# Four engines' instruction streams as hardware loops instead of written out, in a macaron transformer kernel on one core

## The chip, the core and the metric

The kernel runs on one core of a Trainium2 chip. A core has five engines with a program each: TensorE (PE, whose weight loads are listed as PEld), VectorE (DVE), ScalarE (ACT), GpSimd (POOL) and SyncE (SP), which here issues DMAs. They meet only through semaphores: an instruction adds to one when it is done, another waits until it has reached a value. The metric is the device time of one execution in microseconds (us), lower is better. The kernel before took 3411.37 us (median of 3 runs, 3408.09 to 3413.0).

## What is computed

The input `x` is 2 x 1024 tokens of 128 numbers in float32. The reference, cut to what matters:

```python
x = x + 0.5 * ffn_ref(layernorm(x))      # 6 layers, below
x = x + attn_ref(layernorm(x))           # h = x @ w_in.T + b_in; y[t] = sigmoid(a) * y[t-1] + b * h[t]; y @ w_out.T + b_out
x = x + 0.5 * ffn_ref(layernorm(x))      # the same 6 layers again

def ffn_ref(x):
    for i in range(6):
        x = attn_layer(shift_tokens(x), Wqkv[i], q_scale[i], k_scale[i], Wo[i]) + x
        x = ffn_layer(shift_tokens(x), ln_g[i], ln_b[i], W1[i], b1[i], W2[i], b2[i]) + x
```

`shift_tokens` takes the second half of the features from the token before. `attn_layer` projects to q, k and v (16 heads of 64), scales q and k to length 1 by head, multiplies by learned scales, rotates them with a scaled rotary table, and lets each block of 32 tokens attend to itself and the block before it, with a mask and a softmax; the result goes through `Wo`. `ffn_layer` is a layer norm, `W1` to a value and a gate of 341 each, value times gelu(gate), and `W2`.

## The kernel before

The 2048 tokens are 16 tiles of 128, and the 12 layers make 192 tiles of work (`T`; `N` = 96 for each six layers). All layers run through one software pipeline. Its step `s` works on tile `s - lag` in each stage; the lags are `L_X` 0 (the shifted input, transposed), `L_QKV` 1 (projection of q and k, sums of squares, rotation), `L_S` 2 (transposes of q and k, values, scores), `L_SM` 3 (softmax), `L_AV` and `L_WO` 4 (attention times values, output projection), `L_F` 5 and `L_F2` 6 (the feed-forward half). Tile `u` of the next layer enters 16 steps after tile `u` of this one. Around step 96 the recurrence between the two halves is worked in (`middle`, lags 7 to 12).

Each engine has its own function `step(k)`, which emits this engine's instructions for one step in a fixed order; the order and the waits are written by hand. A `Step` object `k` stands for one step. In a step that is written out `k.reg` is None: tile numbers, addresses and the values that waits compare with are constants. In a step of a hardware loop `k.reg` is the loop's register; `k.val` and `k.off` then compute each count and address with register instructions at the place where it is first needed in the loop's body, and keep it for later uses in the same body (`memo`). A few waits are emitted only in written-out steps.

The part of a step that the prediction follows:

- TensorE: `project(k, 1)` and `project(k, 0)` (L503) fill both halves of the PSUM tensor `proj`. Behind the transposes of q and the attention come `project(k, 2)` and `project(k, 3)`. Further on come the output projection (L606), the transposes of the probabilities (L614), `values(k, 1)` and `values(k, 0)` (L509), again into `proj`, the transpose of the next input (L652), `hidden` (L522), the mask (L532) and the scores (L540). `values(k, 0)` waits for `v_ab[2]`, VectorE's last rotation, which reads the same half of `proj`.
- ScalarE: `square` (L705) of projections 1 and 0 into `sq`, Exp of the scores (L718), copies of q and of the attention's result, squares 3 and 2, further copies out of PSUM, and Gelu of the gate (L769). The compiler puts an ACT_TABLE_LOAD ahead of a function where the table at hand doesn't hold it.
- VectorE: from `a_sq[0]` on, `rotate(k, c, ...)` multiplies a projection by `tab` twice, into `swp` (L895) and `rot` (L901). Between these stand the row sum of the softmax (L986), its reciprocal (L995) and the sums of squares (L1000, L1003). The inverse root of these is a chain of small operations that ends in `rn` (L882). Then come hT, value times gate (L1037), the row maximum (L1044), its subtraction (L1047) and the statistics of the layer norm (L1052).
- GpSimd: the power for the layer norm (L1114), the softmax's scaling (L1118), `swp` + `rot` (L1124) and its scaling by `rn` (L1133).
- SyncE: four DMAs each for the shifted `xs` and `xs2`, two for `vb`, and in even steps a chunk of the next layer's `wq` and `wo`.

TensorE runs through `pipeline_by_layer`: a prologue, loops of two steps by layer, and a middle that is written out. The other four run through `pipeline`, which in this kernel writes out every step.

Of the kernel before, what the change touches and what calls it, by code (L numbers as in the profile page):

```python
# [47 lines left out]
FRONT = 6  # L48
UNROLL = 2
MID, MID_END = N - TILES + M_X - 1, N + M_Z  # L50
# [6 lines left out]
def macaron(nc, x_in, w_in, b_in, a_in, b_gain, w_out, b_out, w_qkv, q_scale, k_scale, w_o,  # L57
            ln_g, ln_b, w_1, b_1, w_2, b_2, c_rope, c_mask, c_ident, out):
    with ExitStack() as ctx:
# [221 lines left out]
        def unrolled(eng, step, first, end, between=None):  # L281

            for s in range(first, end):
                step(Step(eng, None, s, {}))
                if between is not None:
                    between(s)

        def looped(eng, step, first, end, layer=None):

            odd = first % 2  # L290
            assert (end - first) % UNROLL == 0
            with eng.Fori(first - odd, end - odd, UNROLL) as i:
                memo = {}
                for j in range(UNROLL):
                    step(Step(eng, i, odd + j, memo, layer))

        def pipeline(eng, step, between=None, mid_end=MID_END, end=T, last=T + L_F2):

            unrolled(eng, step, 0, FRONT, between)
            unrolled(eng, step, FRONT, last)  # L300


        def pipeline_by_layer(eng, step, between=None):
# [59 lines left out]
        def _(sp):  # L363
# [114 lines left out]

            sp.wait_ge(c_zero2, 1)
            pipeline(sp, step, between, mid_end=N + TILES, end=OUT - 1, last=OUT + TILES)  # L480
            sp.wait_ge(d_out, 16 * TILES)
            sp.wait_ge(d_wq, 16 * (CHUNKS * LAYERS + FIRST_Q - W_Q // 2))
# [217 lines left out]
        def _(act):  # L700
# [110 lines left out]
            act.wait_ge(c_zero, 1)  # L811
            act.wait_ge(c_zero2, 1)
            pipeline(act, step, between)


        @block.vector
        def _(dve):
# [269 lines left out]

            dve.wait_ge(c_zero, 1)
            pipeline(dve, step, between, end=OUT - 1)


# [141 lines left out]
```

## Time and profile before

| | |
|---|---|
| median of 3 runs | 3411.37 us |
| the profiled execution | 3411.37 us, of which the span from first to last instruction is 3409.5 |
| TensorE busy | 3280.2 us (96%) |
| VectorE busy | 2808.3 us (82%) |
| ScalarE busy | 2425.1 us (71%) |
| GpSimd busy | 2202.4 us (65%) |
| mean granted TensorE clock | 0.993 of full speed |

Busy time is that of the operations on data. Instructions that only compute registers, branch, wait for a semaphore or issue a DMA are not counted; the view of one source line lists them, with the engine's name and a q (PEldq, DVEq). Where a view names a releaser behind an idle time, it is the instruction whose semaphore ended it; "issue" stands where it shows none.

### The profile page before, as it was taken

The page shows a single profiled execution, that of the slowest core. Times are in us where ns is not written, and L with a number is a line of the kernel's source. Part 1 is how long each engine was busy: PE and PEld are TensorE (multiplying, and loading weights), DVE is VectorE, ACT ScalarE, POOL GpSimd, SP SyncE. Part 2 cuts the span into 40 slices and gives each one's busy share as a digit, 9 for nine tenths or more (in the row PEclk, how much of TensorE's full clock was granted, in tenths as well). Part 3 has the DMA queues.
Part 4 walks back from the last instruction along what each step waited for, and adds up shares of the span by engine and source line. Part 5 has one row for each costly group of instructions (what it writes and reads, how often), then busy time and mean ns, then how long its engine had stood idle before and what let it go on. Part 6 is the DMA issues. An engine that isn't in the chain of part 4 may idle for free. (4 is left out here: it accounts for less than half of the span.)

```text
span 3409.5 us, 154564 instructions
## 1 busy us (share of the span) xinstructions
PE 3280.2 (96%) x63324; PEld 2477.0 (73%) x63515; DVE 2808.3 (82%) x6984; ACT 2425.1 (71%) x3769; POOL 2202.4 (65%) x1422
## 2 busy tenths in 40 slices
PE   6999999999999999999999999999999999999998
PEld 4677777777777777777666777777777777777776
DVE  5788888888888888889999887888888888888885
ACT  2777777777777777777666777777777777777775
POOL 4666666666666666667666666666666666666664
PEclk7999999999999999999999999999999999999999
DMA  3111111111111111111111111111111111111111
GB/s 114 50 45 48 46 48 45 46 48 45 48 46 48 45 49 45 45 48 47 46 41 42 48 45 49 45 48 46 48 45 46 47 45 48 45 48 45 51 49 43
DMA packets 198817, 164.11 MB, mean 48 GB/s; under 512 B 139610, under 2 KB 172525, under 8 KB 198509
## 3 DMA queue, kind: packets, MB, share of 16 engines
q1 hardware_dynamic: 193901, 157.05, 16.8%
q10 hardware_dynamic: 4608, 3.34, 0.3%
q8 instruction: 146, 2.39, 0.3%
q14 instruction: 162, 1.33, 0.1%
HBM read 33.38 MB, written 1.05 MB: 10 GB/s over the span
## 5 line engine op out<-in xcount | busy, mean ns | idle before, releaser
L1124 POOL TENSOR_TENSOR rot<-rot,swp 128x1024 f32<-128x1024 f32 x384 | 907.6, 2364 | 140.3 <-DVE rot L901 140.3
L503 PE MATMUL proj<-wq,xsT 128*128 (+1 forms) x1536 | 778.9, 627 | 76.3 <-DMA wq<-in_L_ffn_Wqkv 37.7
L705 ACT ACTIVATE sq<-proj 128x512 f32<-128x512 f32 x768 | 437.7, 596 | 575.6 <-PE proj L503 565.1
L1133 POOL TENSOR_TENSOR rot<-rot,rn 128x1024 f32<-128x1024 f32 x384 | 724.4, 1908 | 0.0
L1114 POOL TENSOR_TENSOR rt<-rt,half 128x1 f32<-128x1 f32 x192 | 105.3, 548 | 855.6 <-DVE rt L983 855.6
L895 DVE TENSOR_TENSOR swp<-proj,tab 128x512 f32<-128x512 f32 x768 | 524.2, 683 | 53.5 <-issue 34.4
L901 DVE TENSOR_TENSOR rot<-proj,tab 128x512 f32<-128x512 f32 x768 | 519.2, 676 | 2.2 <-PE tps L514 2.2
L514 PEld LDWEIGHTS tps<-idf,rot 128*128 128x128 f32 x3072 | 362.6, 142 | 208.8 <-issue 204.7
L1037 DVE SCALAR_TENSOR_TENSOR hT<-proj,b1c,fg 114x128 f32<-114x128 f32 (+1 forms) x576 | 166.7, 345 | 418.2 <-ACT fg L769 412.2
L1118 POOL TENSOR_TENSOR prob<-prob,rr 128x1024 f32<-128x1024 f32 x192 | 365.4, 1903 | 187.2 <-DVE rr L995 187.2
L503 PEld LDWEIGHTS proj<-wq,xsT 128*128 128x128 f32 x1536 | 260.0, 191 | 311.5 <-issue 242.2
L540 PEld LDWEIGHTS sps<-kT,qT 64*32 64x32 f32 x24576 | 357.4, 106 | 88.7 <-issue 88.5
L514 PE MATMUL tps<-idf,rot 128*128 128x128 f32 x3072 | 401.9, 274 | 4.0 <-POOL rot L1133 2.3
L540 PE MATMUL sps<-kT,qT 64*32 64x64 f32 x24576 | 389.8, 217 | 6.0 <-issue 6.0
L509 PE MATMUL proj<-wq,xsT 128*128 (+1 forms) x768 | 391.2, 604 | 2.5 <-DVE rot L901 2.2
L555 PE MATMUL ops<-pT,vb 64*64 64x32 f32 x12288 | 376.4, 221 | 1.7 <-issue 1.5
L606 PE MATMUL ops<-wo,oT 128*128 (+1 forms) x3072 | 374.6, 276 | 2.4 <-ACT oT L727 2.4
L555 PE MATMUL ops<-pT,va 64*64 64x32 f32 x12288 | 372.1, 219 | 1.2 <-issue 1.1
L606 PEld LDWEIGHTS ops<-wo,oT 128*128 128x128 f32 x3072 | 358.2, 192 | 2.6 <-issue 2.6
L555 PEld LDWEIGHTS ops<-pT,vb 64*64 64x64 f32 x12288 | 327.2, 135 | 34.6 <-issue 34.2
L555 PEld LDWEIGHTS ops<-pT,va 64*64 64x64 f32 x12288 | 328.0, 135 | 1.7 <-issue 1.6
L522 PEld LDWEIGHTS proj<-xnT,w 128*114 128x114 f32 (+1 forms) x2304 | 267.9, 178 | 82.8 <-issue 77.5
(113 smaller groups left out, 5683.5 us busy)
## 6 DMA issues: line engine op xcount, KB each, us to landing
vb<-va SPq DMA_DIRECT2D x192, 384.0 KB, 3.5
vb<-va SPq DMA_DIRECT2D x192, 128.0 KB, 3.4
wq<-in_L_ffn_Wqkv SPq DMA_DIRECT2D x95, 192.0 KB
xs<-Z SPq DMA_DIRECT2D x384, 32.0 KB
xs<-Z SPq DMA_DIRECT2D x384, 28.0 KB
xs<-Z SPq DMA_DIRECT2D x384, 3.8 KB
xs<-Z SPq DMA_DIRECT2D x384, 0.2 KB
wo<-in_L_ffn_Wo SPq DMA_DIRECT2D x94, 64.0 KB
```

The lines of the kernel that those rows point to most:

```text
L503: mm(proj[:, c % 2, :], xsT[:, k.parity(L_QKV), :], wq2[:, bass.ds(w + c * 512, 512)], start=True, stop=True).then_inc(p_qkv[c], 1)
L509: mm(proj[:, c, :], xsT[:, k.parity(L_S), :], wq2[:, bass.ds(w + (4 + c) * 512, 512)], start=True, stop=True).then_inc(p_v[c], 1)
L514: last = tr(tps[:, p, :], rot[:, g * INNER + p * P:g * INNER + (p + 1) * P], idf[:, :])
L540: last = mm(sps[to:to + WIN, ty, p * 64:p * 64 + 64], qT[rows, p, w * WIN:(w + 1) * WIN], kT[rows, p, at:at + 2 * WIN], start=False, stop= ...
L555: last = mm(o4[hp * DH:(hp + 1) * DH, g, :], v, pT[rows, p, to:to + WIN], start=True, stop=True, skip_group_check=True)
L606: last = mm(ops[:, 0, 0:P], oT[:, p, :], wo[:, bass.ds(w + p * P, P)], start=(p == 0), stop=(p == PAIRS - 1))
L705: fn(sq[:, c * 512:(c + 1) * 512], proj[:, c % 2, :], ACT.Square).then_inc(a_sq[c], 1)
L895: v.tensor_tensor(halves(swp[:, c * 512:(c + 1) * 512]), swapped, tab[:, bass.ds(po + (2 * g + 1) * POS * DH, DH)] .rearrange("p (a d) -> ...
L901: v.tensor_tensor(heads(rot[:, c * 512:(c + 1) * 512]), heads(src), tab[:, bass.ds(po + 2 * g * POS * DH, DH)].unsqueeze(1) .to_broadcast( ...
L1118: g_.tensor_tensor(pr, pr, rr[:, :].unsqueeze(2).to_broadcast([P, HEADS, 2 * WIN]), ALU.mult).then_inc(g_nrm, 1)
L1124: g_.tensor_tensor(r, r, swp[:, g * INNER:(g + 1) * INNER], ALU.add).then_inc(g_add[g], 1)
L1133: g_.tensor_tensor(r, r, rn[:, g * HEADS:(g + 1) * HEADS].unsqueeze(2) .to_broadcast([P, HEADS, DH]), ALU.mult).then_inc(g_nm[g], 1)
```

## The change

`pipeline` puts two stretches of steps into hardware loops, with two steps in a loop's body (`UNROLL` = 2). `FRONT` is 6, `MID` 86, `MID_END` 108 and `T` 192. `pipeline_by_layer`, and so TensorE's program, isn't touched. Line numbers behind it grow by 3.

```diff
         def pipeline(eng, step, between=None, mid_end=MID_END, end=T, last=T + L_F2):
 
             unrolled(eng, step, 0, FRONT, between)
-            unrolled(eng, step, FRONT, last)
+            looped(eng, step, FRONT, MID)
+            unrolled(eng, step, MID, mid_end)
+            looped(eng, step, mid_end, end)
+            unrolled(eng, step, end, last)
```

ScalarE and GpSimd loop over steps 6 to 85 and 108 to 191, VectorE over 6 to 85 and 108 to 181 (`end` is `OUT - 1`), SyncE over 6 to 85 and 112 to 181. `looped` was there before, for TensorE:

```python
with eng.Fori(first - odd, end - odd, UNROLL) as i:
    memo = {}
    for j in range(UNROLL):
        step(Step(eng, i, odd + j, memo, layer))
```

With it the instructions on the four engines change. ScalarE at the start of a step, written out (`sq` is the square, `prob` the Exp, `qT` the copy of q):

```order
L705 ACTIVATE sq<-proj 128x512 [waits p_qkv1,v_red0]
L705 ACTIVATE sq<-proj 128x512 [waits p_qkv0]
L718 ACT_TABLE_LOAD
L718 ACTIVATE prob<-prob 128x1024 [waits v_sub]
L723 COPY qT<-tps 128x1024 [waits p_S,p_qT]
```

The same place in the first step of a loop's body, an even step:

```order
L292 ISA
L708 ACT_TABLE_LOAD [waits p_qkv1]
L708 ACTIVATE sq<-proj 128x512 [waits v_red0]
L708 ACTIVATE sq<-proj 128x512 [waits p_qkv0]
L224 REGISTER_ALU
L721 ACTIVATE prob<-prob 128x1024 [waits v_sub]
L726 COPY qT<-tps 128x1024 [waits p_S,p_qT]
```

The table load stands ahead of the first square now, behind the wait for `p_qkv1`, and there is none at the Exp. In the body's second step it stands at the Exp, as before. ISA and REGISTER_ALU are register instructions; an ISA row is a fused one that does several.

ScalarE at the Gelu, written out:

```order
L709 COPY va<-proj 128x512 [waits p_v0]
L769 ACT_TABLE_LOAD [waits v_h]
L769 ACTIVATE fg<-proj,b1c 114x128 [waits p_f1]
L769 ACTIVATE fg<-proj,b1c 114x128
L769 ACTIVATE fg<-proj,b1c 113x128
```

And in the loop:

```order
L712 COPY va<-proj 128x512 [waits p_v0]
L772 ISA [waits v_h,p_f1]
L772 ACT_TABLE_LOAD
L772 ACTIVATE fg<-proj,b1c 114x128
L772 ISA
L772 ACTIVATE fg<-proj,b1c 114x128
```

The wait for `p_f1`, the gate's half of `hidden`, stood behind the table load and stands ahead of it now.

VectorE at the start of a step, from the statistics of the layer norm on, written out:

```order
L1052 BN_STATS st<-xs 128x6 [waits d_xs2]
L895 TENSOR_TENSOR swp<-proj,tab 128x512 [waits g_add0,a_sq0,g_tab]
L901 TENSOR_TENSOR rot<-proj,tab 128x512 [waits p_qT,a_sq0]
L895 TENSOR_TENSOR swp<-proj,tab 128x512 [waits g_add0,a_sq1,v_bn]
L978 BN_AGGR mv<-st 128x2
```

And in the loop, at the body's second step:

```order
L1055 BN_STATS st<-xs 128x6 [waits d_xs2]
L224 REGISTER_ALU [waits g_tab]
L898 ISA [waits g_add0,a_sq0]
L898 ISA
L898 TENSOR_TENSOR swp<-proj,tab 128x512
L904 ISA [waits p_qT,a_sq0]
L904 TENSOR_TENSOR rot<-proj,tab 128x512
L898 TENSOR_TENSOR swp<-proj,tab 128x512 [waits g_add0,a_sq1,v_bn]
```

Between the arrival of `a_sq0` and the first product stand two fused register instructions, which work out the place in `tab`.

## Rows read from the trace of the kernel before

**Rows 1.** The page: busy us by engine, share of the span, instructions.

```profile
PE 3280.2 (96%) x63324; PEld 2477.0 (73%) x63515; DVE 2808.3 (82%) x6984; ACT 2425.1 (71%) x3769; POOL 2202.4 (65%) x1422
```

**Rows 2.** Waits: engine, line, releaser, us in total, times, longest.

```profile
ACT sq L705 <- PE proj L503: 565.1, 413, 6.4
...
DVE swp L895 <- issue: 34.4, 78, 1.1
...
PEld proj L509 <- DVE rot L901: 8.6, 23, 1.1
```

**Rows 3.** TensorE's weight loads in time: start, busy us, idle before; three step starts.

```profile
2004.45 0.30 PEld L503 LDWEIGHTS proj<-wq,xsT 128*128 128x128 f32 x2 [0.27 <-issue]
...
2016.24 0.30 PEld L509 LDWEIGHTS proj<-wq,xsT 128*128 128x128 f32 x2
...
2017.41 1.37 PEld L522 LDWEIGHTS proj<-xnT,w 128*114 128x114 f32 x12 [0.49 <-issue]
2018.78 0.14 PEld L532 LDWEIGHTS sps<-mask,idb 128*128 128x128 bf16 x2
...
2021.84 0.30 PEld L503 LDWEIGHTS proj<-wq,xsT 128*128 128x128 f32 x2 [0.65 <-issue]
...
2038.80 0.30 PEld L503 LDWEIGHTS proj<-wq,xsT 128*128 128x128 f32 x2 [0.27 <-issue]
```

**Rows 4.** ScalarE in time, in the same even step.

```profile
2005.67 0.60 ACT L705 ACTIVATE sq<-proj 128x512 f32<-128x512 f32 x1 [2.32 <-PE proj L503]
2006.47 0.60 ACT L705 ACTIVATE sq<-proj 128x512 f32<-128x512 f32 x1 [0.20 <-PE proj L503]
2007.09 1.28 ACT L718 ACT_TABLE_LOAD   x1
...
2011.32 1.08 ACT L705 ACTIVATE sq<-proj 128x512 f32<-128x512 f32 x2
...
2018.01 1.28 ACT L769 ACT_TABLE_LOAD   x1
```

**Rows 5.** VectorE in time, in that step and at the start of the next.

```profile
2007.16 0.69 DVE L895 TENSOR_TENSOR swp<-proj,tab 128x512 f32<-128x512 f32 x1
...
2010.93 0.25 DVE L995 RECIPROCAL rr<-rs 128x16 f32<-128x16 f32 x1
2011.10 1.17 DVE L1000 TENSOR_REDUCE sps<-sq 128x16 f32<-128x1024 f32 x1
...
2015.38 0.68 DVE L901 TENSOR_TENSOR rot<-proj,tab 128x512 f32<-128x512 f32 x1
...
2017.67 0.19 DVE L882 SCALAR_TENSOR_TENSOR rn<-rt,sps 128x32 f32<-128x32 f32 x1
2020.29 0.87 DVE L1037 SCALAR_TENSOR_TENSOR hT<-proj,b1c,fg 114x128 f32<-114x128 f32 x3 [2.43 <-ACT fg L769]
2021.43 1.23 DVE L1044 TENSOR_REDUCE mx<-sps 128x16 f32<-128x1024 f32 x1 [0.28 <-PE sps L540]
...
2024.55 0.69 DVE L895 TENSOR_TENSOR swp<-proj,tab 128x512 f32<-128x512 f32 x1 [0.43 <-issue]
```

**Rows 6.** ScalarE's table loads at the Exp: count, us busy, mean ns.

```profile
L718 ACT ACT_TABLE_LOAD x189 | 242.5, 1283 | 3.3
```

**Rows 7.** Control instructions of TensorE's queue by source line: count, ns min/median/max.

```profile
L224 PEldq ALU_OP  x640: 32/32/42, 131.6 to 3311.7; - x160
...
L292 PEldq COMPARE_BRANCH  x80: 81/216/262, 166.5 to 3328.3; - x80
...
L532 PEldq FUSED_REGOPS  x160: 107/110/120, 145.9 to 3325.9; - x160
```

**Rows 8.** The page's DMA queues for instructions: packets, MB.

```profile
q8 instruction: 146, 2.39, 0.3%
q14 instruction: 162, 1.33, 0.1%
```

**Rows 9.** A small transfer: KB, us from issue to landing.

```profile
out<-xb SPq DMA_DIRECT2D x16, 64.0 KB, 1.8
```

## The prediction

> **What bounds the kernel now.** I read the views in this order: the page's busy shares, the waits, the order of time of one step on TensorE, the same step on ScalarE and VectorE, and last the rows of the control instructions that the busy shares leave out.
>
> The shares name TensorE: 3280.2 us, 96% of the span [rows 1]. The waits show the others idle, ScalarE for 565.1 us before its squares [rows 2], and VectorE stands 2.43 us before hT in a step [rows 5]. Read so, ScalarE and VectorE have 2 to 3 us to spare in each step and more instructions on them would cost nothing. The step itself says otherwise. TensorE's loads for `project` start at 2004.45, 2021.84 and 2038.80 [rows 3]: 17.39 us for the even step, 16.96 for the odd one, 34.35 a pair. Inside the even step:
> - `project` starts at 2004.45; ScalarE squares its two halves at 2005.67 and 2006.47, each 0.60 long [rows 3, 4]. The second ends at 2007.07.
> - VectorE takes it up at 2007.16, 0.09 later, and 17 more operations run behind it without idle time until the last rotation ends, 2015.38 + 0.68 = 2016.06 [rows 5].
> - TensorE's load for `values(k, 0)`, which must wait for that rotation (its PSUM bank is the one that the rotation reads), starts at 2016.24 [rows 3], 0.18 after it. After it come the transpose, `hidden`, the mask, the scores and the next `project` in a row [rows 3].
>
> So 2.62 + 0.09 + 8.90 + 0.18 = 11.8 us of the 17.4 are a chain over ScalarE and VectorE, and the rest is TensorE's own. The chain closes on itself in every step. TensorE looks busy only because its own work over those 11.8 us (projections, transposes, attention, output projection) happens to be as long as the chain; it has hardly any wait there to give (8.6 us in 23 waits of L509 for the rotation) [rows 2]. A microsecond added between a `project` and the last rotation is a microsecond on the period. ScalarE's and VectorE's idle times lie elsewhere: 2.32 us before the first square, in which ScalarE can do nothing for this tile, and the 2.43 us before hT.
>
> The Trainium skill ("Perfetto Trace Analysis", "Identifying the Most-Contended Engine") says to take the engine of highest occupancy as the one that binds, and, for TensorE, to distrust the matmul share. By its first half a change that leaves TensorE's program alone leaves 3411 us; this trace disagrees, by the 0.18 us between the rotation and the load.
>
> **The change part by part.** TensorE's program stays the same. Steps 6 to 85 (40 turns of two steps) and from 108 on become loops: 42 turns on ScalarE and GpSimd, 37 on VectorE, 35 on SyncE, whose second loop starts at 112. The prologue, the middle (22 steps around the recurrence, 26 on SyncE) and the last steps stay written out.
>
> 1. *The table load changes place.* Written out, ScalarE loads a table before each Exp (189 loads of 1283 ns) and one before each Gelu [rows 4, 6]; Square follows Gelu without one. At 2007.09 to 2008.37 the Exp's load lies behind both squares, and the row sum that waits for Exp comes late enough not to see it. In the loop the first instruction with a function is the Square of the even step; the program order puts a load there, behind the wait for `p_qkv1`, and none before the Exp of that step. In the odd step the load stays at Exp. So in 42 + 40 = 82 even steps the first square starts 1.28 us later. The second used to wait for its half until 2006.47, 0.80 after the first; back to back it follows by about 0.49 (two squares take 1.08 us) [rows 4]. Its end moves by 1.28 + 0.02 + 0.49 - 0.80 = 1.0 us. This lies on the chain: 1.0 x 82 = 82 us.
>
> 2. *Control instructions in front of VectorE's first product.* In the loop the `tab` offset is worked out behind the wait for `a_sq0`: two fused register instructions, then `swp`. Nothing covers them, since all else waits for the same square. No row of VectorE has such an instruction. Nearest are TensorE's: ALU_OP 32 ns, the fused one for the mask 110 ns, a compare-and-branch 216 [rows 7]. The two here compute several values each, as the 110 ns one does. With a little for the passage from one to the next I take 0.15 each, 0.3 us a step, in even and odd steps.
>
> 3. *Control instructions behind the row sum.* In the even step the count for `g_nrm` is computed behind the wait for `v_sum`, and a fused instruction stands between the reciprocal and the first reduction (2010.93 and 2011.10) [rows 5]. The reciprocal lasts 0.25, so it hides about one of the three. I take 0.28. In the odd step the counts are known: 0.
>
> 4. *Those that are covered.* The address and count instructions before the other products and reductions lie under operations of 0.68 to 1.22 us; the loop's back edge (the branch is 0.22 on TensorE, the whole turn 0.65 - 0.27 = 0.38 before its loads) [rows 3, 7] on VectorE lies under L1047's operation, which is as long as L1044's 1.23 us [rows 5], and on ScalarE in its 2.32 us of idleness [rows 4]. In the rsqrt chain an operation of 0.19 us waits for the one before; one register instruction fits beside each, and the three around the Z update add some 0.4 us to rn (2017.67 + 0.19 = 2017.86) [rows 5]. The mask's load is at 2018.78 [rows 3], 0.9 later, so 0.4 is covered; if each cost 0.22 it would be 0.9 and just show.
>    ScalarE's Gelu load now stands behind the wait for `p_f1` and not before it: it ran at 2018.01, while `hidden` ran from 2017.41 [rows 3, 4]. It moves by about 0.4, hT by 0.6 with its own fused instructions. hT ended at 2020.29 + 0.87 = 2021.16, its follower began at 2021.43, so 0.3 comes through to L1047 and BN_STATS. In the even step the later square covers that; in the odd one VectorE was idle 0.43 us before `swp` [rows 5]. Cost 0, with 0.1 us to spare.
>    GpSimd is busy for 65% of the span and late nowhere on the chain, and SyncE's ten DMA issues of a step have whole steps until they are read, so their address instructions cost nothing; without that cover theirs would be about 0.1 us each on xs2.
>
> Sum: even 1.0 + 0.3 + 0.28 = 1.58, odd 0.3, a pair 1.88, with 0.9 of it from VectorE. 82 x 1.0 + 77 x 0.9 = 82 + 69 = 151 us. The profiled execution took 3411.37 us, 1.9 more than its span, and is itself the median of the runs. 3411 + 151 = **3562 us**, 4.4% slower.
>
> Bounds: seven control instructions of a pair are exposed (two, two, and three). At 0.032 us (an ALU_OP) they are 0.2 a pair, at 0.216 (the branch) 1.5: 82 + 15 = 97 to 82 + 116 = 198 us, 3508 to 3609. I lie between, near the fused rows, since most of these are fused. Below nothing they can't be: they are added ahead of the same operation.
>
> **The rivals.**
> - *Code is fetched again in every turn.* Written out, the four engines' code comes once over q14 (162 packets, 1.33 MB), and TensorE's over q8 [rows 8]. TensorE's loops turn 80 times [rows 7] and q8 moved only 2.39 MB, so its loops stay in place once fetched. VectorE's body has 122 rows in the order, and semaphore waits beside them, more than one of q14's packets (8 KB) may hold. If its fetch ran anew in each turn, it would be like a small transfer, 1.8 us from issue to landing [rows 9], with 1.23 us of L1047 as cover: 0.6 x 77 = 46 us, and up to 1.8 x 77 = 139. Time 3562 + 90 = 3650. Against it: TensorE's loops. The Trainium skill ("Advanced Engine Details and Errata", "ISA Cache") gives two lines of 256 instructions for these engines. By that rule the body, which spans two lines at most, stays in; the 8 KB packets here suggest smaller lines, and then it could lie in three. 12%.
> - *The load hides in ScalarE's idle time.* If ScalarE did the load in the 2.32 us before the square, term 1 would be gone and 69 us stay: 3480. Against it: the order has the wait ahead of the load. 6%.
> - *Nothing comes through, and less code helps (the other side).* One mechanism: the load hides as above, and the control instructions are done ahead while the engine waits for the square. Decisive is whether they run before `a_sq0` arrives; from there on each costs. What is left is a gain: 34.4 us of idle time before `swp` has no engine as its cause [rows 2]; if that were slow issue from code that is fetched for the first time, loops would return it: 3377 to 3411. Against: the 0.43 us before `swp` at 2024.55 is TensorE's own back edge (0.65 against 0.27 us before `project`) [rows 3, 5], which stays. 3%.
> - *TensorE binds after all*, as the shares say: 3411. 2%.
> - *The same mechanism at other sizes*: operands and waits in registers cost something on each instruction, and the covers of point 4 give way. Each 0.1 us a step is 15 us; 3600 to 3640. 10%.
>
> **How the numbers follow.** The forecast has the remaining 67%, with 3508 to 3609 as its own range. For 8 in 10 the range goes down to 3490, a little under term 1 alone (3493), and up to 3645, which takes in the larger sizes and about half of the fetch case. A measurement of this kernel can tell about 0.2% from no change, 7 us. Faster 0.02, same 0.02, slower 0.96.
>
> **What the profile after would show.** A group of 82 table loads at the first square's line with the Exp's cut to about 107; in even steps 3.6 us from `project`'s start to the end of the second square (2.62 now); 0.35 to 0.45 us from there to `swp` (0.09 now) in both; periods of 19.0 and 17.3 us; TensorE's share at 92%, waits of L509 and L503 for the rotation in place of 8.6 us, and the 22 middle steps as before. Periods that stay under 18 in even steps refute term 1; idle time on VectorE without a cause that comes once in two steps, and a q14 that moves as much as before or more, would show the fetch rival. If the odd steps grew by more than 0.6 us, I have missed a cover.

## The result

| | before | after |
|---|---|---|
| median, same chip | 3412.18 us (4 runs, 3408.09 to 3413.89) | 3538.03 us (4 runs, 3534.35 to 3539.02) |
| ratio to before | | 1.0369, 95% interval 1.0351 to 1.0386 |
| profiled execution, its span | 3411.37, 3409.5 us | 3532.97, 3531.2 us |
| mean granted TensorE clock | 0.993 | 0.994 |

The kernel became 3.7% slower: 126 us by the medians, 121.6 by the two profiled executions, against 151 forecast.

### The profile page after: what moved, and what is told of

It reads as the page before. It is cut to its first block and busy times, and to the rows that moved or that the text cites. A ratio compares the mean times of both kernels' runs of the same rounds, so it can differ in the third digit from the quotient of the medians.

```text
span 3531.2 us, 163209 instructions
## 1 busy us (share of the span) xinstructions
PE 3342.1 (95%) x63324; PEld 2469.2 (70%) x63515; DVE 2822.3 (80%) x6984; ACT 2419.0 (69%) x3769; POOL 2203.2 (62%) x1422
## 3 DMA queue, kind: packets, MB, share of 16 engines
q8 instruction: 146, 2.39, 0.3%
## 5 line engine op out<-in xcount | busy, mean ns | idle before, releaser
L506 PE MATMUL proj<-wq,xsT 128*128 (+1 forms) x1536 | 806.2, 636 | 110.6 <-issue 38.6
L506 PEld LDWEIGHTS proj<-wq,xsT 128*128 128x128 f32 x1536 | 248.0, 190 | 388.2 <-issue 315.9
L512 PE MATMUL proj<-wq,xsT 128*128 (+1 forms) x768 | 408.8, 616 | 17.2 <-DVE rot L904 1.9
```

Source lines behind the costliest of these rows:

```text
L506: mm(proj[:, c % 2, :], xsT[:, k.parity(L_QKV), :], wq2[:, bass.ds(w + c * 512, 512)], start=True, stop=True).then_inc(p_qkv[c], 1)
L512: mm(proj[:, c, :], xsT[:, k.parity(L_S), :], wq2[:, bass.ds(w + (4 + c) * 512, 512)], start=True, stop=True).then_inc(p_v[c], 1)
```

## The profile after

The page, with the busy row that answers to [rows 1] and the instruction queues that answer to [rows 8]:

```profile
PE 3342.1 (95%) x63324; PEld 2469.2 (70%) x63515; DVE 2822.3 (80%) x6984; ACT 2419.0 (69%) x3769; POOL 2203.2 (62%) x1422
...
q8 instruction: 146, 2.39, 0.3%
q14 instruction: 36, 0.29, 0.0%
```

No engine has an instruction more on data than before. TensorE's busy time nevertheless grew by 62 us with the same 63324 matmuls: a busy share holds time in which a matmul stands and waits. It is not a measure of work. q14 fell from 162 packets to 36.

The waits (engine, line, releaser, us in total, times, longest); the first, the third and the last answer to [rows 2], and line numbers are higher by 3:

```profile
ACT sq L708 <- PE proj L506: 523.5, 477, 6.6
...
ACT L708 <- PE proj L506: 79.7, 39, 2.8
...
DVE swp L898 <- issue: 69.2, 80, 2.2
DVE swp L898 <- ACT sq L708: 68.4, 80, 4.9
...
PE proj L506 <- DVE rot L904: 38.0, 43, 4.5
...
PE sps L535 <- issue: 17.1, 77, 0.7
...
PEld proj L512 <- DVE rot L904: 9.4, 24, 1.1
```

The second row has no output name: it is the table load itself, which now waits for TensorE in the square's place, 39 times. The row of L535 is new: 77 times, once in each turn of VectorE's loops, the mask's matmul waits. The last row stands nearly as it did (8.6 us in 23 times): the wait at the last rotation, which closes the chain, shows in this view as little as before, although the chain grew. The fifth row did grow, by 30 us. In the kernel before it was

```profile
PE proj L503 <- DVE rot L901: 8.2, 4, 4.5
```

The new waits are 0.72 us each and come once in an even step of the first loop: a later `project` of that step waits there for a rotation.

One even step and the odd one behind it, on TensorE's load queue (start, us, idle before), to be laid beside [rows 3]:

```profile
1135.58 0.30 PEld L506 LDWEIGHTS proj<-wq,xsT 128*128 128x128 f32 x2 [0.27 <-issue]
...
1148.94 0.30 PEld L512 LDWEIGHTS proj<-wq,xsT 128*128 128x128 f32 x2 [0.47 <-issue]
...
1151.61 0.11 PEld L535 LDWEIGHTS sps<-mask,idb 128*128 128x128 bf16 x2 [0.16 <-issue]
...
1154.65 0.30 PEld L506 LDWEIGHTS proj<-wq,xsT 128*128 128x128 f32 x2 [0.65 <-issue]
```
```profile
1171.99 0.30 PEld L506 LDWEIGHTS proj<-wq,xsT 128*128 128x128 f32 x2 [0.27 <-issue]
```

The starts of `project` lie 19.07 and 17.34 us apart, where they lay 17.39 and 16.96 apart.

ScalarE in the same two steps, as [rows 4]:

```profile
1136.79 1.28 ACT L708 ACT_TABLE_LOAD   x1 [2.01 <-PE proj L506]
1138.08 1.09 ACT L708 ACTIVATE sq<-proj 128x512 f32<-128x512 f32 x2
1139.05 1.06 ACT L721 ACTIVATE prob<-prob 128x1024 f32<-128x1024 f32 x1
...
1155.88 0.60 ACT L708 ACTIVATE sq<-proj 128x512 f32<-128x512 f32 x1 [2.53 <-PE proj L506]
1156.67 0.60 ACT L708 ACTIVATE sq<-proj 128x512 f32<-128x512 f32 x1 [0.19 <-PE proj L506]
1157.29 1.28 ACT L721 ACT_TABLE_LOAD   x1
```

In the even step the load starts where the square would have, 1.21 after `project`, and the squares come back to back, so they end at 1139.17, 3.59 after `project`. In the odd step nothing has changed. VectorE, as [rows 5]:

```profile
1138.07 0.28 DVE L1055 BATCH_NORM_STATS2 st<-xs 128x6 f32<-128x128 f32 x1
1139.72 0.69 DVE L898 TENSOR_TENSOR swp<-proj,tab 128x512 f32<-128x512 f32 x1 [1.36 <-issue]
...
1148.13 0.68 DVE L904 TENSOR_TENSOR rot<-proj,tab 128x512 f32<-128x512 f32 x1
...
1149.93 0.29 DVE L1028 TENSOR_TENSOR Z<-Z,ops 128x128 f32 x1 [0.36 <-issue]
...
1150.90 0.19 DVE L885 SCALAR_TENSOR_TENSOR rn<-rt,sps 128x32 f32<-128x32 f32 x1
...
1157.74 0.69 DVE L898 TENSOR_TENSOR swp<-proj,tab 128x512 f32<-128x512 f32 x1 [0.72 <-ACT sq L708]
```

`swp` starts at 1139.72, 0.55 behind the second square (0.09 before), and in the odd step at 1157.74, 0.47 behind it. The control instructions that stand there, by source line (count, ns min/median/max), and a loop's branch on VectorE and TensorE:

```profile
L898 DVEq FUSED_REGOPS  x462: 57/64/323, 116.7 to 3286.0; - x154
```
```profile
L1028 DVEq FUSED_REGOPS  x308: 53/181/310, 127.6 to 3291.4; - x154
```
```profile
L292 PEldq COMPARE_BRANCH  x80: 81/216/258, 169.2 to 3449.4; - x80
...
L292 DVEq COMPARE_BRANCH  x77: 50/56/67, 151.7 to 3297.3; - x77
```

The longer of the two fused instructions that work out the place in `tab` takes up to 323 ns, three times the 110 ns of TensorE's fused row [rows 7], from which I had taken 150.

Where the 121 us are, by the start of `project` in steps 10, 86, 109, 182 and 192 (us between them):

| steps | before | after | difference |
|---|---|---|---|
| to 10 | 184.2 | 187.4 | +3.2 |
| 10 to 86, first loop | 1307.0 | 1385.1 | +78.1 |
| 86 to 109, written out | 427.4 | 425.9 | -1.5 |
| 109 to 182, second loop | 1257.0 | 1297.2 | +40.2 |
| 182 to 192, written out | 170.0 | 171.2 | +1.2 |

Both loops lose, but the first loses twice as much. The mean over the steps of each stretch shows by what (us, even step / odd step):

| stretch of a step | before, 10 to 85 | after, first loop | after, second loop |
|---|---|---|---|
| `project` to end of second square | 2.62 / 2.62 | 3.60 / 2.62 | 2.62 / 2.62 |
| from there to `swp` | 0.09 / 0.11 | 0.55 / 0.47 | 0.55 / 0.47 |
| `swp` to end of last rotation | 8.92 / 8.91 | 9.09 / 8.91 | 9.09 / 8.91 |
| last rotation to the mask's load | 2.72 / 2.59 | 2.82 / 2.60 | 2.82 / 2.62 |
| period | 17.41 / 16.99 | 19.11 / 17.34 | 18.14 / 17.41 |

The 0.11 is 0.09 in 36 of the 38 odd steps and 0.44 in two; what follows counts from 0.09. What is left of a period lies between the mask's load and the next `project`.

In the second loop the squares are as early as ever. ScalarE's table loads by line tell why:

```profile
L708 ACT ACT_TABLE_LOAD  x40: 1283/1283/1283, 114.2 to 1537.9; - x40
```
```profile
L721 ACT ACT_TABLE_LOAD  x149: 1283/1283/1283, 135.5 to 3497.6; - x149
```

40 loads stand at the square, all of the first loop (the last at 1537.9); 149 stayed at Exp, and 40 + 149 are the 189 of [rows 6]. Before the first loop the last table loaded on ScalarE is that of a Sigmoid in step 5, while from the loop's back edge one comes with Gelu's. The two entries don't agree, and so the Square in the body gets a load of its own. The second loop is entered behind a Gelu, both ways hold the same table, and none is needed.

## The experiments

### Is it a chain, and has VectorE room? `op_on_chain`, `op_in_gap`

Two kernels, each the kernel before with one more product of 128x512 on VectorE in each step, on a scratch tile that nothing reads. Once it stands between the first `swp` and the first `rot`, once ahead of the wait for hT:

```diff
+                    v.tensor_tensor(dum[:, 512:1024], dum[:, 0:512], dum[:, 0:512], ALU.mult)
                     rotate(k, 0, False)
...
                 if k.on(L_F):
+                    v.tensor_tensor(dum[:, 512:1024], dum[:, 0:512], dum[:, 0:512], ALU.mult)
                     k.wait(p_f[0], L_F)
```

Expected of the one on the chain:

> The kernel before, with one more VectorE product of 128x512 into a scratch tile in every step, between the first swp and the first rot, on the chain from a_sq0 to the last rotation (the pitch of such a product is 0.60 us). Chain theory: every one of 192 steps grows by 0.60, 3412 + 115 = 3527 us. TensorE-bound theory: nothing, 3412.

Measured: 3520.49 us, ratio 1.0316 (1.0300 to 1.0332). In the step, `swp` to the last rotation grew by 0.60, and the starts of `project` came 0.56 later each:

```profile
1096.36 0.30 PEld L504 LDWEIGHTS proj<-wq,xsT 128*128 128x128 f32 x2 [0.65 <-issue]
...
1113.92 0.30 PEld L504 LDWEIGHTS proj<-wq,xsT 128*128 128x128 f32 x2 [0.27 <-issue]
...
1131.94 0.19 PEld L504 LDWEIGHTS proj<-wq,xsT 128*128 128x128 f32 x1 [0.65 <-issue]
```

17.56 and 18.02 us, where an odd and an even step took 17.0 and 17.4. Time behind the squares is paid nearly whole by the step, with VectorE at 82% of the span.

Expected of the one in the gap:

> The kernel before, with the same product in front of the wait for hT, where VectorE stood idle for 2.43 us. Chain theory: 3412, within 0.3%, though VectorE does 115 us more. A theory by VectorE's total work: as much as on the chain, 3527.

Measured: 3432.14 us, 1.0058 (1.0043 to 1.0074), 20 us more than nothing. The pipelined steps did not move (means 17.40 and 16.98 in steps 10 to 85). All of it lies in the steps 86 to 109 that hold the recurrence, 450.0 us instead of 427.4. The view of one stretch there (us, and busy us of PE, PEld, DVE, ACT, POOL; then the granted TensorE clock, the DMA engines' share and GB/s), of the kernel before:

```profile
1500.00:1880.00 380.00, 357.06 (x6688) 267.05 (x6707) 369.80 (x903) 257.58 (x412) 254.78 (x189) 1.00 0.17 45
```

VectorE is busy 369.80 of 380 us there, so in the middle there was hardly any room for more of its work. The same view over the steps 86 to 109 alone, for the kernel before, `op_in_gap` and `op_on_chain`:

```profile
1491.27:1918.66 427.39, 403.34 (x7651) 302.41 (x7670) 409.52 (x998) 292.73 (x465) 285.30 (x210) 1.00 0.17 45
```
```profile
1491.10:1941.10 450.00, 414.08 (x7650) 308.91 (x7671) 435.28 (x1021) 293.23 (x465) 296.72 (x210) 0.97 0.16 43
```
```profile
1539.70:1979.50 439.80, 407.38 (x7651) 301.61 (x7670) 423.37 (x1021) 292.87 (x465) 285.69 (x210) 1.00 0.16 44
```

On the chain VectorE's busy time grew by 13.9 us there and the time by 12.4, 0.54 us a step. In the gap they grew by 25.8 and 22.6, 0.98 us a step. But in the gap TensorE's granted clock fell too, to 0.97 in the mean: in seven stretches of 3.4 us it stood at the lower of its two levels, 1.2 GHz, where it did so in one before and in none with the product on the chain. If all that TensorE lost by this came through, it would be 7 x 3.4 / 2 = 12 us, by my estimate. So what the product cost in the middle is not cleanly VectorE's, and the runs don't part the two. In the pipelined steps it cost nothing before hT, and on the chain 0.56. There the place decides and not the amount, which the share of busy time can't show; but my expectation of no cost had left the middle out.

The added product itself was not of one length. By source line (count, ns min/median/max), on the chain and in the gap:

```profile
L973 DVE TENSOR_TENSOR dum<-dum x192: 679/682/1867, 16.8 to 3457.3; 128x512 f32<-128x512 f32 x192
```
```profile
L1032 DVE TENSOR_TENSOR dum<-dum x192: 680/1273/2334, 110.2 to 3424.1; 128x512 f32<-128x512 f32 x192
```

In the gap it took nearly double, in the median. The pipelined steps had room even for that. One of these products on VectorE, and GpSimd beside it:

```profile
1074.36 1.27 DVE L1032 TENSOR_TENSOR dum<-dum 128x512 f32<-128x512 f32 x1
```
```profile
1075.04 0.91 POOL L1101 TENSOR_TENSOR tab<-rope,scl 128x128 f32<-128x128 f32 x1
```

GpSimd's operation lasted 0.91 us there and 0.46 in the median of the kernel before. On the chain 190 of the 192 products stood beside no operation of GpSimd and took 0.68 us. In the gap 167 stood beside this pair, `tab` and the sum of `rot` and `swp`, with 1.27 in the median, while 12 that met only GpSimd's power `mrs`, in the middle, and 4 that met nothing took 0.68. So the two engines, each working on SBUF alone, seem to slow one another; this is read from the overlap.

### Which engine's loop costs? `dve_alone`, `dve_written`, `pool_sp_alone`

The changed kernel, with some engines kept as written-out steps: ScalarE, GpSimd and SyncE in `dve_alone`, VectorE in `dve_written`, VectorE and ScalarE in `pool_sp_alone`. For one engine the edit is:

```diff
+        def written(eng, step, between=None, mid_end=MID_END, end=T, last=T + L_F2):
+            unrolled(eng, step, 0, FRONT, between)
+            unrolled(eng, step, FRONT, last)
...
-            pipeline(act, step, between)
+            written(act, step, between)
```

> Of the change, VectorE's loops alone; ScalarE, GpSimd and SyncE written out. Theory: the register work on the chain is VectorE's alone, 0.75 us in even and 0.35 in odd steps for 77 turns, so 83 us, less what the covers give: 3412 + 78 to 85 = 3490 to 3497. Rival (half of it comes from ScalarE's moved Gelu load or the others' register work): 3450 to 3475.

Measured: 3497.89 us, 1.0255 (1.0239 to 1.0271): +86. Periods 18.13 / 17.35 in the first loop.

> ScalarE, GpSimd and SyncE in loops, VectorE written out. Theory: only the table load before the first square of the even steps of the first loop is left on the chain: 40 turns x 0.98 = 39 us, 3412 + 39 = 3451, with even steps of the first loop at 18.4 us, all others as before. Rival: VectorE's instructions and the table load share a cover, and each alone costs less or more than in the sum (VectorE alone gave +85): 3412 + 126 - 85 = 3453 for additive; below 3440 or above 3465 for not.

Measured: 3450.39 us, 1.0111 (1.0095 to 1.0126): +39. Even steps of the first loop 18.32, its odd ones 16.97, the second loop 17.41 / 17.03, as before.

> GpSimd's and SyncE's loops alone. Theory: both are off the chain by more than their register work, 3412, within 0.2%. Rival: their later DMAs and later g_nrm come through, 0.1 us or more a step, 3430.

Measured: 3412.48 us, 1.0000 (0.9991 to 1.0009): 0.

The parts add up: 86 + 39 + 0 = 125 of the 126 us. VectorE's loop is two thirds of the loss, ScalarE's table load the rest, and it is paid in 40 even steps: 39 / 40 = 0.98 us each, the shift of the second square that the table of stretches shows. GpSimd's and SyncE's loops cost nothing.

### Is it the table at the loop's entry? `sigmoid_early`

The changed kernel, with the Sigmoid issued in the step in which its input is ready, so that Exp and Gelu follow it before the loop is entered:

```diff
+                    fn(siga[:, :], rawT[:, RAW_C + 1:RAW_C + 2], ACT.Sigmoid).then_inc(c_sig, 1)
                 if s >= PREPARE:
...
-                if s == FRONT - 1:
-                    fn(siga[:, :], rawT[:, RAW_C + 1:RAW_C + 2], ACT.Sigmoid).then_inc(c_sig, 1)
```

> The changed kernel, with the one Sigmoid ahead of the first loop moved two steps earlier, ahead of a Gelu, so that the loop is entered with Gelu's table and the Exp's load stays at the Exp in both steps of the body. Theory of the table load: 40 even steps lose 0.98 us each, 3538 - 39 = 3499. Rival (the load hides in ScalarE's idle time, and the even steps of the first loop are long for another reason, such as fetched code): 3538.

Measured: 3495.42 us, 1.0245 (1.0231 to 1.0259), 43 below the changed kernel. An even step of the first loop on ScalarE:

```profile
1109.25 0.60 ACT L708 ACTIVATE sq<-proj 128x512 f32<-128x512 f32 x1 [2.04 <-PE proj L506]
1110.04 0.60 ACT L708 ACTIVATE sq<-proj 128x512 f32<-128x512 f32 x1 [0.20 <-PE proj L506]
1110.65 1.28 ACT L721 ACT_TABLE_LOAD   x1
```

The load is back behind both squares, where it is hidden, though all is still in loops. One instruction of step 5, outside the loop, decided over 40 us inside it.

### Is it the register instructions ahead of swp? `offset_early`, `bits`

`offset_early` is the changed kernel with a tiny operation ahead of the wait for the square that uses the place in `tab`. The place is then worked out while VectorE would only wait:

```diff
+                    if k.reg is not None:
+                        po = k.off("pos", L_QKV, lambda u: (u % POS) * DH + ((u // TILES) % 2) * (4 * POS * DH))
+                        v.tensor_scalar(dum[:, 0:1], tab[:, bass.ds(po + POS * DH, 1)], 1.0, None, ALU.mult)
                     rotate(k, 0, True)
```

> The changed kernel, with a one-column VectorE operation that uses the tab offset put ahead of the wait for a_sq0, so that the two fused register instructions run while VectorE waits. Theory of register work on the chain: the distance from the second square to swp falls from 0.47 to 0.55 us to about 0.1 in 77 turns of two steps, 3538 - 77 x 0.83 = 3474. Rival (the delay is the loop's own, by branch or code fetch): even steps keep their 0.55, odd ones fall, 3538 - 30 = 3508 or more.

Measured: 3477.5 us, 1.0190 (1.0176 to 1.0203), 60 below the changed kernel, with an operation more. VectorE in an odd step:

```profile
1113.84 0.28 DVE L1059 BATCH_NORM_STATS2 st<-xs 128x6 f32<-128x128 f32 x1
1114.04 0.14 DVE L977 TENSOR_SCALAR dum<-tab 128x1 f32 x1
1114.80 0.69 DVE L899 TENSOR_TENSOR swp<-proj,tab 128x512 f32<-128x512 f32 x1 [0.63 <-ACT sq L709]
```

The releaser of `swp` is the square again, at 0.04 us behind it in the mean (0.47 in the changed kernel); the period fell to 16.93 us, even a little under the kernel before. In even steps it is 0.03 in the first loop but 0.36 in the second: there VectorE is still at the statistics of the layer norm when the square is done (they end 0.38 us behind it).

`bits` asks what in these instructions is dear. It is the changed kernel with the place in `tab` and the slot of `Z` by bit masks in place of remainders and divisions:

```diff
-                po = k.off("pos", L_QKV, lambda u: (u % POS) * DH + ((u // TILES) % 2) * (4 * POS * DH))
+                po = k.off("pos", L_QKV, lambda u: (u & (POS - 1)) * DH + (u & TILES) * (4 * POS * DH // TILES))
...
+                if bits[0]:
+                    return self.off(("slot", back, part), lag,
+                                    lambda u: (u & (TILES - 1)) * P + (u & POS) * (P // POS) + (1 - back) * P + part)
                 return self.off(("slot", back, part), lag,
                                 lambda u: (u % TILES + (u // POS) % 2 + 1 - back) * P + part)
```

`bits[0]` is set ahead of VectorE's program, and holds for GpSimd's behind it too.

> The changed kernel, with the place in tab (all VectorE) and the slot of Z (VectorE and GpSimd) worked out by bit masks in place of remainders and a division. The same values; the table load stays where it is. Theory: the 0.32 us of the fused instruction before swp are its two remainders and its division, so with masks the passage from the end of the second square to swp falls from 0.55 and 0.47 us to about 0.3, the same instruction in front of the Z operations shrinks too and the mask's load comes nearer to rn: 0.2 us a step on the chain, 77 x 2 x 0.2 = 31 us, 3538 - 31 = 3507. Rival: what costs is the number of instructions behind the wait (with masks there are as many or more): 3538, or slower by some us.

Measured: 3539.58 us, 1.0373 (1.0359 to 1.0387): no gain at all. My theory fell. At the line of `swp` there now stand

```profile
L903 DVEq ALU_OP  x462: 45/45/57, 118.2 to 3287.4; - x154
L903 DVEq FUSED_REGOPS  x308: 57/114/165, 118.5 to 3292.2; - x154
```

In an odd step that is three single ones of 45 ns, started 0.075 us apart, and a fused one of 157 ns. From the start of the first to the end of the last it is 0.382 us, against 0.389 for the 294 ns and the 64 ns instruction that stood in the same step of the changed kernel. `swp` follows the square by 0.53 / 0.47 us, as in the changed kernel (0.55 / 0.47). Remainders and a division are no dearer here than masks; the time seems to go with the number of arithmetic steps in the formula, which is seven in the one form and six in the other by the source, at some 0.06 us each (an estimate). That reading fits both kernels, but no run varied the number alone.

### Both fixes, and masks with one of them: `both_fixes`, `bits_sigmoid`

`both_fixes` has the edits of `sigmoid_early` and `offset_early`, `bits_sigmoid` those of `bits` and `sigmoid_early`.

> The changed kernel with both repairs: the Sigmoid moved early, and the tab offset used ahead of the wait. Theory: they are independent, except in the second loop and now in the first, where ScalarE's Gelu load behind its wait leaves VectorE busy until 0.36 us after the square in even steps. 3538 - 43 - 60 + 40 x 0.32 = 3448; if they simply add, 3435.

Measured: 3446.28 us, 1.0099 (1.0084 to 1.0115). Apart the two gave 43 and 60 us, together 92 and not 103. In even steps of the first loop `swp` came 0.03 us behind the square with the table load in place, and comes 0.28 behind it without: once the square is early, VectorE is the late one (its statistics end 0.31 us behind the square). The 0.25 us more in 40 steps are 10 us, about what is missing from the 103. This is the cover of which point 4 of the prediction speaks.

> The kernel of bits, and Sigmoid moved from the step before the first loop to the step in which its input is ready. Adds: 3538 - 31 - 43 = 3464 if the masks give 31; 3495 if they give nothing.

Measured: 3498.88 us, 1.0257 (1.0243 to 1.0271): 41 below `bits`, and the masks give nothing here either.

### The other way: TensorE written out too, `pe_written`

The kernel before, with TensorE's loops unrolled as well:

```diff
+            unrolled(eng, step, 0, FRONT, between)
+            unrolled(eng, step, FRONT, T + L_F2)
+            return
             at = L_F + UNROLL
-            unrolled(eng, step, 0, at, between)
```

> The kernel before with TensorE written out too. Theory: TensorE's back edge delays project by 0.42 us in 80 odd steps, all of it on the chain: 3412 - 80 x 0.42 = 3378. Rival: the code of TensorE, now fetched throughout, comes too slowly, and the time stays at 3412 or grows.

Measured: 3403.14 us, 0.9975 (0.9964 to 0.9985), the fastest of all, though by 8 us only and not 34. Its instruction queues, and five starts of `project` in a row:

```profile
q8 instruction: 509, 8.34, 1.0%
...
q14 instruction: 162, 1.33, 0.1%
```
```profile
1040.43 0.30 PEld L505 LDWEIGHTS proj<-wq,xsT 128*128 128x128 f32 x2
...
1057.26 0.30 PEld L505 LDWEIGHTS proj<-wq,xsT 128*128 128x128 f32 x2
...
1073.98 0.30 PEld L505 LDWEIGHTS proj<-wq,xsT 128*128 128x128 f32 x2
...
1091.27 0.30 PEld L505 LDWEIGHTS proj<-wq,xsT 128*128 128x128 f32 x2
...
1108.01 0.30 PEld L505 LDWEIGHTS proj<-wq,xsT 128*128 128x128 f32 x2
```

The back edge is gone: no idle time ahead of these loads, and the shortest steps take 16.83 and 16.72 us, which is the gain that I expected. But only 43 of the steps 10 to 85 stay under 17 us; the others take up to 18.35, at irregular distances, and the mean is 17.11 against 17.20 before. TensorE's code over q8 grew from 2.39 MB to 8.34 at the same time. In the steps 10 to 85 there are nine idle times of 0.8 to 1.4 us ahead of a load for the scores, of which the kernel before has none; every one ends 2.3 to 3.0 us after a packet of q8 started and 1.6 to 1.8 before the next does. That makes it likely that the long steps wait for code, but it is not shown: no run changed the fetch alone.

## Why the prediction was right

The sign and the place were right: the chain over ScalarE and VectorE sets the step, and what was added between `project` and the last rotation came through, with TensorE's program untouched. The sum came within 30 us because two terms were too large, by 43 and 8 us, and two too small, by 19 and 9. That it lies so near is in part luck.

| term | forecast | measured |
|---|---|---|
| 1, table load ahead of the square | 82 x 1.0 = 82 us | 40 x 0.98 = 39 us |
| 2, register instructions ahead of `swp` | 77 x 0.6 = 46 | 77 x (0.46 + 0.38) = 65 |
| 3, behind the row sum | 77 x 0.28 = 22 | 77 x 0.18 = 14 |
| 4, covered ones | 0 | 77 x (0.11 + 0.01) = 9 |
| sum | 151 | 127; the profiled executions differ by 121.6 |

The measured terms come to about 6 us more than the time, some 0.04 us a step. Some 4 of these lie in the stretch that the table above leaves out, from the mask's load to the next `project`: it got shorter, from 3.06 to 3.05 (even) and 2.76 to 2.74 us (odd) in the first loop and from 3.07 to 3.04 and 2.83 to 2.79 in the second. Why is open.

- **The chain.** `op_on_chain` and `op_in_gap` show it. The rival that TensorE binds after all is refuted: it is busy for 96% of the span, its program didn't change, and the time rose by 3.7%. The Trainium skill ("Perfetto Trace Analysis", "Identifying the Most-Contended Engine") takes the engine of highest occupancy, but has TensorE judged by its weight loads and its FLOPs and not by its matmuls' busy time. By the weight loads' 73% it would be VectorE here, with 82%. The traces don't bear this out in the pipelined steps either: there a product more on VectorE cost 0.56 us or nothing, by its place.
- **Term 1** was mis-sized, by its count. Size and mechanism were right: the second square ends 0.98 us later where the load stands (1.0 forecast), and `sigmoid_early` and `dve_written` give 43 and 39 us for it. The step that failed is "so in 42 + 40 = 82 even steps": I took the order of one loop's body for both. The order of the second loop, or the Sigmoid in step 5, would have shown that the load belongs to the first loop's entry. What the runs showed in its place is 40 loads, all in the first loop. This is also not the rival "the load hides in ScalarE's idle time", since in the first loop nothing hides.
- **Term 2** was too small. Each fused instruction was taken at 0.15 us from TensorE's 110 ns [rows 7]; the one with most arithmetic takes about 0.3. The two steps cost 0.46 and 0.38 and not 0.3. `offset_early` gave back 60 of these 65 us. The upper bound of two times 0.216 was passed too in the even step (0.46 against 0.43): the branch was the dearest control row at hand, but it holds one operation and says nothing of a formula with seven.
- **Term 3** was 0.18 instead of 0.28, from the mean over the even steps. Of it 0.12 lie between the row sum and the first reduction, the rest elsewhere in the stretch.
- **Point 4.** GpSimd's and SyncE's instructions cost nothing, as `pool_sp_alone` shows. The cover at the mask gave way by a little: `rn` ends 0.48 us later behind the last rotation (2.28 instead of 1.80; 0.4 forecast), and the mask's load follows it by 0.54 instead of 0.91. I had taken all of the 0.9 as slack. Behind `rn` the mask's load seems to need some 0.5 us in these even steps, so the slack was 0.4. The new wait of 17.1 us in 77 times on L535 fits this. The move of Gelu's load stayed hidden in the changed kernel. Once the other terms are gone VectorE is late by 0.36 us ahead of `swp` (`offset_early`, second loop). Part of this seems to be ScalarE's: in even steps there VectorE's statistics end 0.01 us behind the square in `dve_alone` and 0.24 in the changed kernel. No run moved Gelu's load alone.
- **Code fetched anew in each turn** is refuted: q14 moved 36 packets and not 162 or more. The Trainium skill ("Runtime: NRT & Kernel Launch", "Instruction fetch mechanics") says that a taken branch out of the window of two pages forces a fetch, and that full unrolling is to be preferred. No run here shows such a fetch: the loops fetched less, and it is the written-out TensorE, with the most fetched, whose steps became uneven.
- **Of the signs named,** the count of 82 loads was wrong (40). 3.6 us to the second square holds (3.60). Periods of 19.0 and 17.3 hold in the first loop (19.11, 17.34); in the second they are 18.14 and 17.41. 0.35 to 0.45 us ahead of `swp` was 0.55 and 0.47. TensorE's share was to fall to 92% and stayed at 95. Of the waits for the rotation those at L509 did not grow (9.4 us); those of `project`'s matmuls did (8.2 to 38.0). Beside these waits the records of its matmuls took time in, 62 us more for the same matmuls, 56 of them at `project`, `values` and `hidden`. The middle took 425.9 us against 427.4, as forecast.

## What to carry to other kernels

Look for the chain before the shares: follow one tile through the engines and compare the closed path with the period; an instruction costs where that path goes through it, and nothing where it fits into a wait of its engine for something else. When steps become a hardware loop, price what the compiler now puts behind waits: the register arithmetic at each first use, and a table load that is needed only because the loop's entry and its back edge hold different tables. Both can be moved off the path while the loop stays, by using the operand once ahead of the wait and by entering the loop behind the function that its body ends with; here that took back 92 of 126 us, and left the loops still 1% behind the code written out.

## What the runs showed of the hardware

- A fused register instruction on VectorE took 46 to 323 ns. The same address by remainders or by masks took 0.389 or 0.382 us in all. A single one took 40 to 45 ns on VectorE, 32 on TensorE and GpSimd, 35 on ScalarE (medians).
- A loop's branch took 56 ns on VectorE and 216 on TensorE (medians). The Trainium skill ("Advanced Engine Details and Errata", "Control Flow Timing") gives some 108 ns for a compare-and-branch and names no engine; both measured values lie off it by a factor of two, to either side.
- The four looped engines' code came over q14 in 36 packets (0.29 MB) instead of 162 (1.33 MB), and no run shows time given back by it: GpSimd and SyncE in loops took 3412.48 against 3411.52 us.
- The same product of SBUF operands took 682 ns on VectorE (median) at a place where GpSimd stood still in 190 of 192 cases, and 1273 where GpSimd was at work, whose own operation beside it doubled too (0.91 us, 0.46 before). No run moved GpSimd's work alone, so the cause is read from the overlap.
- With VectorE's product in the gap TensorE's granted clock was 0.97 over the steps 86 to 109, where it was 1.00 without it; TensorE was busy for 414.08 of 450.00 us there and for 403.34 of 427.39 before.
